# Window scores head by head, one plain copy of the transposed q, and the mask written by ScalarE

## The reference

```python
WINDOW, HEADS, DIM_HEAD = 32, 16, 64
q, k = l2norm(q) * qs, l2norm(k) * ksc                 # then rotated by position (cos, sin, scale)
bq  = q.reshape(b, h, nw, w, d)                        # windows of 32 queries
bk2 = look(k)                                          # 64 keys: the window before and the own one
mask = (it < jb) | (it > jb + w) | (jb == -1)
sim = einsum('bhwie,bhwje->bhwij', bq, bk2) * 8.0
sim = where(mask, -finfo.max, sim)
out = einsum('bhwij,bhwje->bhwie', softmax(sim), look(v))
x = out_of_heads @ Wo + x
x = (a * gelu(gate)) @ W2 + b2 + x                     # a, gate = split(layernorm(x) @ W1 + b1)
```

## Time and profile before

| | |
|---|---|
| median of 3 runs | 3803.61 us (3802.78 to 3813.33) |
| the profiled execution, its own time | 3801.54 us |
| its span in the trace | 3799.7 us |
| mean granted clock of TensorE | 0.933 |
| busy share PE, PEld, DVE, ACT, POOL | 85%, 73%, 79%, 68%, 66% |

### The profile page before, as it was taken

The page is one execution under the profiler, slowest core; times in us unless marked ns, Lnnn a source line. Parts: engine busy times, 40 slices in busy tenths (PEclk is TensorE's granted clock), DMA queues, the critical chain, the costliest instruction groups (busy, mean ns, idle before and its releaser), DMA issues.

```text
span 3799.7 us, 126632 instructions
## 1 busy us (share of the span) xinstructions
PE 3233.2 (85%) x52674; PEld 2775.9 (73%) x52674; DVE 3009.8 (79%) x4462; ACT 2600.9 (68%) x3787; POOL 2503.0 (66%) x2289
## 2 busy tenths in 40 slices
PE   3444447999989999989999899999899998999996
PEld 2333236788878888778888788888788887888885
DVE  5766767888888788888788887888887888888883
ACT  2222235777777778778787777787687777788775
POOL 1000007887777778778787777887787787788772
PEclk8666668999999999999999999999999999999997
DMA  1000001111111111111111111111111111111111
GB/s 57 0 0 0 0 0 35 37 55 33 33 34 39 57 35 36 36 35 38 57 36 35 30 41 59 36 35 36 34 38 53 36 36 35 37 37 40 30 35 32
DMA packets 54638, 129.97 MB, mean 34 GB/s; under 512 B 10944, under 2 KB 28864, under 8 KB 53312
## 3 DMA queue, kind: packets, MB, share of 16 engines
q1 hardware_dynamic: 54080, 122.02, 11.0%
HBM read 19.25 MB, written 2.10 MB: 6 GB/s over the span
## 4 chain that ended last, share of the span: by engine, by line
PE 56%; DVE 17%; issue 11%; ACT 11%; POOL 5%; DMA 0%; SPq 0%; POOLq 0%; ACTq 0%; DVEq 0%
PE pair L214 44%; PE pair L217 12%; ACT qT L736 6%; POOL qk L959 3%; DVE ss L860 2%; DVE ts L856 2%; DVE pair L873 1%; DVE den L908 1%; ACT sq L726 1%; DVE qk L852 1%; ACT sq L718 1%; POOL Sx L991 1%; DVE qT L359 1%; DVE mx L877 1%; DVE VA L344 0%
## 5 line engine op out<-in xcount | busy, mean ns | idle before, releaser
L980 POOL TENSOR_TENSOR qk<-qk,ts 128x1024 f32<-128x1024 f32 x384 | 910.9, 2383 | 218.8 <-DVE ts L856 205.0
L959 POOL TENSOR_TENSOR qk<-qk,rn 128x1024 f32<-128x1024 f32 x384 | 734.0, 1932 | 43.6 <-issue 28.8
L852 DVE TENSOR_TENSOR qk<-pair,tab 128x1024 f32<-128x1024 f32 x384 | 468.7, 1221 | 370.3 <-ACT sq L718 368.2
L214 PE MATMUL pair<-wq_h,xs_h 128*128 128x512 f32 x1154 | 515.7, 447 | 36.5 <-issue 18.6
L217 PE MATMUL pair<-small,qk 128*128 128x128 f32 x3192 | 452.4, 285 | 79.0 <-ACT qT L736 40.4
L217 PEld LDWEIGHTS pair<-small,qk 128*128 128x128 f32 x3192 | 360.2, 145 | 168.4 <-issue 96.0
L991 POOL TENSOR_TENSOR Sx<-Sx,rden 128x1024 f32<-128x1024 f32 x192 | 365.7, 1905 | 157.3 <-DVE rden L911 157.3
L856 DVE TENSOR_TENSOR ts<-pair,tab 128x1024 f32<-128x1024 f32 x384 | 466.7, 1215 | 0.0
L214 PE MATMUL pair<-wq_h,xs_l 128*128 128x512 f32 x1152 | 465.0, 404 | 0.0
L860 DVE TENSOR_REDUCE ss<-sq 128x16 f32<-128x1024 f32 x384 | 464.6, 1210 | 0.0
L713 ACT ACTIVATE Sx<-Sx 128x1024 f32<-128x1024 f32 x192 | 203.7, 1061 | 378.0 <-DVE Sx L881 378.0
(11 more groups left out here) (201 smaller groups left out, 7079.4 us busy)
## 6 DMA issues: line engine op xcount, KB each, us to landing
VB<-VA SPq DMA_DIRECT2D x192, 384.0 KB, 3.5
VB<-VA SPq DMA_DIRECT2D x96, 128.0 KB, 3.5
wq_raw<-wqkv SPq DMA_DIRECT2D x6, 1536.0 KB, 8.4
xf<-xT SPq DMA_DIRECT2D x96, 64.0 KB, 1.9
xf<-xT SPq DMA_DIRECT2D x96, 63.8 KB, 2.0
wo_sb<-wo SPq DMA_DIRECT2D x6, 512.0 KB, 3.7
out<-X SPq DMA_DIRECT2D x8, 256.0 KB, 2.3
w_raw<-fw SPq DMA_DIRECT2D x6, 341.0 KB, 8.3
```

The source lines that it names most:

```text
L214: return T_.matmul(out, lhsT, rhs, start=start, stop=stop, **k)
L852: V_.tensor_tensor(h3(qk[:, now, kind, :], DH), h3(source[:, :], DH), rep(tab[:, 2 * kind, b, :], HEADS, DH), ALU.mult)
L959: G_.tensor_tensor(x, x, bc(rn[:, then, kind * HEADS:(kind + 1) * HEADS], HEADS, DH), ALU.mult).then_inc(S["scaled"], 1)
L980: G_.tensor_tensor(qk[:, now, kind, :], qk[:, now, kind, :], ts[:, kind, :], ALU.add).then_inc(S["added"], 1)
```

## The change

The copy of q becomes one instruction over 128 partitions and keeps the transposes as they are; the zeros go. The scores are then done for each head by itself: a matmul over the 64 partitions of that head, with 32 queries as weights, and its output in 32 partitions of PSUM. The mask is written by ACT, between the copy of the AV result and the copy of k, and DVE writes none.

```diff
-        qT = sb("qT", [P, PAIRS, 4, 2 * WIN])
+        qT = sb("qT", [P, PAIRS, P])
@@ step_pe
-                            last = mm(PB[w * KEYS:(w + 1) * KEYS, to:to + KEYS], qT[:, a, 2 * pair + w, :],
-                                      kT[:, a, key0:key0 + KEYS], False, True, skip_group_check=True)
+                            q0 = (2 * pair + w) * WIN
+                            for odd in range(2):
+                                rows = slice(odd * DH, (odd + 1) * DH)
+                                at = w * KEYS + odd * WIN
+                                last = mm(PB[at:at + WIN, to:to + KEYS], qT[rows, a, q0:q0 + WIN],
+                                          kT[rows, a, key0:key0 + KEYS], False, True, skip_group_check=True)
@@ step_act
-                for odd in range(2):
-                    rows = slice(odd * DH, (odd + 1) * DH)
-                    last = A_.activation(qT[rows, :, :, odd * WIN:(odd + 1) * WIN],
-                                         PC[rows, :].rearrange("p (a w q) -> p a w q", a=PAIRS, w=4), ACT.Copy)
-                last.then_inc(S["qkT_kept"], 1)
+                A_.activation(qT[:, :, :], h3(PC[:, :], P), ACT.Copy).then_inc(S["qkT_kept"], 1)
...
             if pl.has(1):
+                bb = (t - 1) % BLOCKS
+                if pl.has(3):
+                    e.wait_ge(S["o_kept"], blocks(pl, "o_kept", 3, 1))
+                elif pl.has(2):
+                    e.wait_ge(S["shifted"], blocks(pl, "shifted", 2, 1))
+                else:
+                    e.wait_ge(S["opened"], 1)
+                A_.activation(h3(PB[:, :], P), rep(mask[:, bb * P:(bb + 1) * P], PAIRS, P), ACT.Copy).then_inc(S["masked"], 1)
                 e.wait_ge(S["qkT_done"], blocks(pl, "qkT_done", 1, 2))
-                bb = (t - 1) % BLOCKS
                 A_.activation(kT[:, :, WIN + bb * P:WIN + (bb + 1) * P], h3(PC[:, :], P), ACT.Copy).then_inc(S["qkT_kept"], 1)
@@ step_dve
-            def write_mask(back):
-                ...
-                V_.tensor_copy(h3(PB[:, :], P), rep(mask[:, bb * P:(bb + 1) * P], PAIRS, P)).then_inc(S["masked"], 1)
...
                 rotate(1, other)
-                write_mask(1)
                 square_sums(1)
@@ clear
-            V_.memset(qT[:, :, :, :], 0.0)
```

More of the change, by code:

```diff
@@ L192, in build @@
         lane_small = [x[:, k, :] for x in (sq, ts) for k in range(2)]
-        lane_stats = flat(qT[:, :, :, :])
+        lane_stats = flat(qT[:, :, :])
         vec_half = sb("vec_half", [P, 1])
@@ L901, in step_dve @@
                 rotate(1, other)
-                write_mask(1)
                 square_sums(1)
-            else:
-                write_mask(1)
             if pl.has(2):
```

## The result

The changed kernel takes 3929.8 us (median of 4 runs, 3922.4 to 3932.0), the kernel before 3808.5 us on the same chip (3802.8 to 3815.9). The ratio is 1.032, with a 95% interval of 1.030 to 1.035: slower, 33 us above the 3897 predicted and inside the range. The profiled execution took 3922.4 us.

What follows compares the result with a forecast made beforehand. PE was taken to set the pace. 3801.5 us + 34 (order on ACT) + 43 (late packets) + 20 (lost q cover) - 2 (zeroing) = 3897 us, 2.5% slower; range 3830 to 3990.

Steps and rivals of the forecast that it cites:

- The order on ACT: ACT's mask ahead of k's copy makes PE wait at `xf` in odd steps: +0.40 us a pair, +34 us.
- The prediction's pair of 31.51 us: An odd and an even step together take 31.51 us after the change, against 31.11 before.
- The pace of the scores: PE's scores: 128 records on four tiles take 1.9 us at AV's pace; no change was taken.
- The rival with eight tiles: PE's scores flow by eight tiles, 128 records in 0.93 us: pair 30.98 us, total 3775 us; chance 0.08.
- the one without overlap: PE's small tiles don't overlap, 29 ns a record, scores take 3.7 us: total about 4130 us; chance 0.07.
- the estimate of 3.2 us: PE's scores by the skill page's 60 cycles of overhead per matmul: 25 ns a record, 3.2 us.
- DVE's relief: DVE writes no masks, so the odd step's maximum starts some 0.49 us earlier: gain 0.47 us per even step.
- The lost cover of the q copy: AV's gaps no longer hide behind PE's wait for q (0.3 to 0.4 us each), at some 50 gaps: +20 us.
- The packets: Late instruction packets stop PE: 51 us more in scores, 10 in AV; 0.7 of 61 reaches the end, +43.
- - 2: The zeroing of `qT` at the start goes away, saving about 2 us once.

Runs made afterwards that it cites:

- kernel 8: The changed kernel with 64 score records of the old shape in place of 128: 3833.4 us, ratio 1.008 to the kernel before.
- Kernel 1: The changed kernel with ACT's copy of k ahead of the mask: 3855.0 us, ratio 1.014 to the kernel before.
- kernels 7 and 2: Kernel 2: the changed kernel with the mask back on DVE, 3844.7 us; kernel 7: the same with 64 score records of the old shape, 3778.5 us.

## Why the prediction was right, and where it was off

**The order on ACT: right.** The prediction's pair of 31.51 us is kernel 8's 31.50, though the 0.01 is luck: over all its steps without a stop, from AV to AV, the medians add up to 31.47. It stands for 33 of the 34 us predicted. Kernel 1 shows what it hangs on: with k's copy ahead, the wait at `xf` is gone, and with it 1.9% of the time.

**The pace of the scores: right.** 128 records take 1.93 us to the next matmul, 1.99 by their row, where 64 had 2.09 in theirs; that is 15 ns a record, and 1.9 us was forecast. (The rival with eight tiles names a pair of 30.98 us; by its own numbers, 0.93 less than 31.51, it is 30.58, and its 3775 us stand.) The rival with eight tiles (0.93 us) and the one without overlap (3.7 us) are excluded by that row. So is the estimate of 3.2 us that I had worked out from the Trainium skill, TensorEngine Tiling (Array Packing), Instruction Overhead: its 60 cycles for each matmul don't add up where four tiles are in use. Its advice not to split a small dimension held here for another reason, the instructions that must be brought.

**DVE's relief: worth its place in the pair, no more.** It was costed inside the 31.51.

**The lost cover of the q copy, +20 us: the right mechanism, too large, and unseen in the time.** The wait for q did hide a part of each stop, but 0.26 us and not 0.3 to 0.4, and at 49 AV bursts: 11 us by the lengths of AV in the kernel before and in kernel 8. Kernel 8's whole 32 us are used up by the order on ACT, so that no run shows that even the 11 reach the end.

**The packets, 0.7 of 61 us = +43: the right cause, mis-sized.** The idle time at AV and scores grew by 112.5 - 51.2 = 61.3 us, the 61 predicted, but half of it in AV (31) and half in the scores (31), not 10 and 51. I took the row for the price of a stop. Each stop costs up to 0.29 us more than its row, and about all of it reached the end, not 0.7: 68.3 us of idle in 80 more stops is 91 us, and 91 (give or take 12) is what the change stands above kernel 8. My 0.7 was read off the kernel before, where DVE and L945 hold back the next maximum. It fits kernels 7 and 2, where the mask stays on DVE (0.72 by this count, 0.8 by the lengths of the bursts). That the relief of DVE is why the share rose to 1 in the changed kernel is argued from these two pairs of kernels, was not tried by itself, and is within the noise by the second count.

With the sizes measured, and no cover, the sum is 3801.5 + 33 + 91 - 2 = 3923.5 us for a profiled execution of 3922.4. The 91 is itself the distance between two of the times, so this closeness is no proof. Against it the prediction had 48 us too little for the packets and 20 too much for the cover, which cancel in part; that the forecast came within 33 us owes something to this. The rest of the 33 us is that this execution was the fastest of the four.

## What to carry to other kernels

Count instructions as well as work: two bursts that each issue 256 instructions in under 2 us cost PE more in stops than the whole rearrangement of ACT did. When a burst stops with nothing to wait for, at the same records in every pass of a loop, look where the packets of the instruction queue end, and shift the program before changing the algorithm: some 500 tiny matmuls, which compute nothing, made the tuned kernel 1.1% faster. And when an instruction moves to another engine, ask what stands behind it there: the mask behind k's copy cost nothing, the mask ahead of it 1.3%.

## What the runs showed of the hardware

The change adds 12,288 records and their loads, 24,576 instructions of PE, and 100 packets to the instruction queue: 256 instructions (96 packets) explain nearly all of them. By the DMA view of the kernel before, the packet ahead of the stop of the earlier trace rows moves at 2042.9, and takes 3.5% of 16 engines' 2 us, about 1.1 us of one; AV goes on at 2045.27, some 2.4 us after.

```profile
GB/s 0 0 0 0 0 0 0 0 0 0 0 0 0 0 0 0 0 0 328 0 0 0 0 0 0 0 0 0 0 0 0 0 0 0 0 0 0 0 0 0
...
q8 instruction: 1, 0.02, 3.5%
```

A burst of 256 instructions in 1.8 to 1.9 us stops when a limit lies late in it; one of 128 in 2 us showed no stop, in the steps from 630 us on of any kernel here. That the packet's way of 2.4 us is what the burst outruns is my reading of this one place. Also new to me: 64 semaphore increments on PE cost 8.7 us, 136 ns each, some nine times a small record.
